# First pass of a graph kernel on Trainium2: ScalarE's norm of the older group ahead of the newer group's root, VectorE's statistics ahead of the scores

## The chip, the cores and the metric

The kernel runs on one core of one Trainium2 chip. Its engines are TensorE (PE), VectorE (DVE), ScalarE (ACT), GpSimd (POOL) and SyncE (SP); each takes its own instructions strictly in their order, and they meet only at semaphores. ACT, POOL and SP also issue DMA transfers. The metric is the device time of one execution in microseconds (us); the time before is the median of three runs.

## The reference, cut to what matters

```python
# x: (50000, 256) f32, 12500 edges (src, dst), dst sorted
h = einsum(x, W); a_src = sum(h * att_src); a_dst = sum(h * att_dst)
e = leaky_relu(a_src[src] + a_dst[dst])            # per edge and head
alpha = softmax of e over the edges with the same dst
gat = relu(segment_sum(h[src] * alpha, dst) + bias)
x1 = layernorm(x + gat)                            # all 50000 rows
for l in range(3):                                 # edges only: 12500
    e = relu((x1[dst] - x1[src]) @ theta.T + x1[src] @ phi.T)
    agg = segment_max(e, src); x1' = relu(batchnorm(agg))
out = layernorm(x1 + x1')
```

Most of the 50000 rows have no edge that ends in them. For these gat is relu(bias), and x1 is layernorm(x + relu(bias)). The first pass computes that for all rows; rows with edges are overwritten later.

## The kernel before

The rows of x are worked in 40 groups, numbered 0 to 39: 39 of 1280 rows (a tile of 128 partitions x 10 rows x 256 features, 1280 KB) and one of 80 rows. The edges are worked in 25 tiles of 512 (`NS` = 25). The part of the program that the change touches runs from about 108 to 404 us, and interleaves the two.

Edge tile t: POOL gathers its dst and src rows with 8 indirect DMAs (L835, function `gat_pool`) into one of two buffers; PE transposes them (L850, `turn`), ACT copies the four banks to SBUF (L879, `gat_keep`), PE multiplies them to the scores (L862, logits) and to h (L868), DVE copies the scores out of PSUM (L895, `gat_score`), SP stores them (L903), and ACT copies h (L888, `gat_keep_h`). PE runs `turn(t+1)` and then the products of tile t; the products of tile t wait for the score copy of tile t - 1, since both use bank 4. POOL may fill a buffer for tile t when tile t - 2 has been transposed (and its dst rows stored by SP).

Row group g: `pre_stats` on DVE waits for the group's load, adds the bias (L778, 128x2560), takes ten bn_stats (L781) and ten bn_aggr (L787). `pre_std` on ACT takes the root (L795). `pre_finish` on DVE makes the inverse root with a Newton step and the shift (L804 to L812). `pre_turnover` on ACT norms the ten rows (`pre_norm`, L820), issues the store (L713) and then the load (L699) of a later group into the ring. Groups 4 to 11 lie in the big buffer and were loaded at the start. All others pass a ring of four buffers: from group 12 on, the turnover of group g issues the load of group g + 3, so the load of group g + 1 goes out behind the norm of group g - 2. The load waits for the store of group g - 1, the ring buffer's last user; the issuing engine, ACT, does that wait.

The order is written out by hand. Step t of the loop pairs edge tile t with group 4 + t: group 28 goes with tile 24, the last. On ACT a step s holds `gat_keep(s)`, `gat_keep_h(s-1)`, `pre_std(4+s-1)` and `pre_turnover(4+s-2)`, so the root of a group stands ahead of the norm of the group before it. On DVE a step t holds `gat_score(t)`, `pre_finish(4+t-1)` and `pre_stats(4+t)`:

```python
            for t in range(NS):
                gat_score(dve, t)
                if t:
                    pre_finish(dve, PRE_SORT + t - 1)
                pre_stats(dve, PRE_SORT + t)
```

After the last tile the scores go to DRAM and back (L903, L935), and DVE runs the softmax over all edges (from L964 on), with groups 29 to 33 put between its pieces, then groups 34 to 39; after that comes the message stage, in which POOL scatters the finished rows (L1123). These parts follow the loop in the same order on every engine.

Of the kernel before, what the change touches and what calls it, by code (L numbers as in the profile page):

```python
# [21 lines left out]
NS = -(-E // SUP)  # L22
# [29 lines left out]
PRE_SORT = 4  # L52
# [7 lines left out]
def gnn(nc, x, src, dst, w, att_src, att_dst, bias, theta_t, phi_t, gammas, betas, out):  # L60
    ctx = ExitStack()
    with ctx:
# [272 lines left out]
        def in_big(g):  # L335

            return PRE_SORT <= g < PRE_SORT + PRE_BIG

        def ring_use(g):

            return g if g < PRE_SORT else g - PRE_BIG
# [7 lines left out]
        def pre_rows(g):  # L349
            if in_big(g):  # L350
                lo = NS * 2 * SUP - (PRE_SORT + PRE_BIG - g) * PR * D
                return big[:, lo:lo + PR * D].rearrange("p (r f) -> p r f", r=PR)
            return pre[:, ring_use(g) % PRE_RING, :, :]

        def loaded(e, g):
            if in_big(g):
                e.wait_ge(s_big_x[(g - PRE_SORT) * 2 // PRE_BIG], 16)
            else:
                e.wait_ge(s_pre_x[ring_use(g) % PRE_RING], 16 * (ring_use(g) // PRE_RING + 1))
# [7 lines left out]
        def node_rows(g):  # L367

            if g == PG:
                return slice(PG * P * PR, N), PTAIL, 1  # L370
            return slice(g * P * PR, (g + 1) * P * PR), P, PR
# [321 lines left out]
        def pre_load(a, use):  # L693
            g = group_at(use)
            rows, p, r = node_rows(g)
            b, u = use % PRE_RING, use // PRE_RING
            if u:
                a.wait_ge(s_pre_stored[b], 16 * u)
            a.dma_start(pre[0:p, b, 0:r, :], x[rows, :].rearrange("(p r) f -> p r f", r=r)).then_inc(s_pre_x[b], 16)  # L699
# [9 lines left out]
        def pre_store(a, g):  # L709
            rows, p, r = node_rows(g)  # L710
            stored = s_big_stored[g - PRE_SORT] if in_big(g) else s_pre_stored[ring_use(g) % PRE_RING]
            a.wait_ge(s_pre_normed, g + 1)
            a.dma_start(x1_dram[rows, :].rearrange("(p r) f -> p r f", r=r), pre_rows(g)[0:p, 0:r, :]).then_inc(stored, 16)  # L713
# [48 lines left out]
        def newtons(g):  # L762

            return 5 * g if g <= PRE_SORT else 5 * PRE_SORT + 4 * (g - PRE_SORT)
# [8 lines left out]
        def pre_stats(v, g):  # L773
            rows, p, r = node_rows(g)
            e, c = g % 2, g - PRE_SORT
            y = pre_rows(g)[0:p, 0:r, :]
            loaded(v, g)
            v.tensor_tensor(y, y, rbias_ps[0:p, :].unsqueeze(1).to_broadcast([p, r, D]), ALU.add).then_inc(s_pre_sum, 1)  # L778
            v.wait_ge(s_pre_sum, c + 1)
            for n in range(r):  # L780
                m = v.bn_stats(stat[0:p, e, n, :], y[:, n, :])  # L781
            m.then_inc(s_pre_stat, 1)
            v.wait_ge(s_pre_stat, c + 1)
            if g > 1:
                v.wait_ge(s_pre_std, g - 1)
            for n in range(r):
                m = v.bn_aggr(mv[0:p, e, n, :], stat[0:p, e, n, :])  # L787
            m.then_inc(s_pre_mv, 1)

        def pre_std(a, g):  # L790
            rows, p, r = node_rows(g)
            e = g % 2
            a.wait_ge(s_pre_mv, g - PRE_SORT + 1)
            a.wait_ge(s_pre_newton, newtons(g - 1))
            a.activation(std[0:p, e, 0:r], mv[0:p, e, 0:r, 1], ACT.Sqrt, bias=eps_b[0:p, :]).then_inc(s_pre_std, 1)  # L795
# [18 lines left out]
        def pre_norm(a, g):  # L814
            rows, p, r = node_rows(g)
            b = g % PRE_RING
            a.wait_ge(s_pre_shift, 2 * g + 2)
            for n in range(r):
                o = pre_rows(g)[0:p, n, :]
                m = a.activation(o, o, ACT.Identity, scale=inv[0:p, b, n:n + 1], bias=shift[0:p, b, n:n + 1])  # L820
            m.then_inc(s_pre_normed, 1)
# [50 lines left out]
        def gat_keep(a, t):  # L872
            par = t % 2
            if t > 1:
                a.wait_ge(s_logits, t - 1)
                a.wait_ge(s_h_done, 2 * (t - 1))
            for n in range(4):
                a.wait_ge(s_row_turned, 4 * t + n + 1)
                a.activation(turned[:, par, 1 - n // 2, n % 2, :], bank[n], ACT.Copy).then_inc(s_row_kept, 1)  # L879
# [10 lines left out]
        def gat_score(v, t):  # L890
            par = t % 2
            v.wait_ge(s_logits, t + 1)
            if t > 1:
                v.wait_ge(s_score_stored[par], 16 * (t // 2))
            v.tensor_copy(score[:, par, :], bank[4][0:H, :]).then_inc(s_score, 1)  # L895
# [637 lines left out]
        @block.sync  # L1533
        def _(sp):
            setup_sync(sp)
            big_load_sync(sp)
            lists_sync(sp)
            soft_masks_sync(sp)
            for s in range(NS + 1):
                if s < NS:  # L1540
                    xd_store(sp, s)
                if 1 <= s <= NS:
                    score_store(sp, s - 1)
            soft_in_sync(sp)
            alpha_sync(sp)
            theta_sync(sp)
            in_steps([(0, lambda t: msg_load(sp, t))], NS)
            for l in range(L):
                conv_sync(sp, l)
            final_sync(sp)  # L1550
            dense_sync(sp)
# [12 lines left out]
        @block.scalar  # L1564
        def _(act):
            act.wait_ge(s_ids, 32)
            for use in range(PRE_SORT):
                pre_load(act, use)
            act.wait_ge(s_const, CONST)

            def pre_turnover(g):
                pre_norm(act, g)
                pre_store(act, g)
                if not in_big(g) and ring_use(g) and ring_use(g) - 1 + PRE_RING < RING_USES:
                    pre_load(act, ring_use(g) - 1 + PRE_RING)
            rows_sum_act(act, 0)
            rows_square_act(act, 0)
            for g in range(1, PRE_SORT):
                rows_sum_act(act, g)
                pre_turnover(g - 1)  # L1580
                rows_square_act(act, g)
            pre_turnover(PRE_SORT - 1)
            act.wait_ge(s_params, PARAMS)
            for s in range(NS + 2):
                if s < NS:
                    gat_keep(act, s)
                if 1 <= s <= NS:
                    gat_keep_h(act, s - 1)
                    pre_std(act, PRE_SORT + s - 1)
                if 2 <= s:  # L1590
                    pre_turnover(PRE_SORT + s - 2)
            for g in range(EARLY, PG + 1):
                if g == EARLY + 2:
                    soft_exp_act(act)
                pre_std(act, g)
                pre_turnover(g)
            msg_act(act)
            for l in range(L):
                conv_act(act, l)
                norm_act(act, l)  # L1600
            final_act(act)
            dense_act(act)

        @block.vector
        def _(dve):
            keys_dve(dve)
            row_bias_dve(dve)
            sort_dve(dve)
            lists_dve(dve)
            rows_finish(dve, PRE_SORT - 1)  # L1610
            rbias_dve(dve)
            weights_dve(dve)
            first_dve(dve)
            for t in range(NS):
                gat_score(dve, t)
                if t:
                    pre_finish(dve, PRE_SORT + t - 1)
                pre_stats(dve, PRE_SORT + t)
            g = EARLY
            soft_flags_dve(dve)  # L1620
            soft_rows_dve(dve)

            def one_group():
                nonlocal g
                pre_finish(dve, g - 1)
                pre_stats(dve, g)
                g += 1
            soft_max_1(dve)
            one_group()
            soft_max_2(dve)  # L1630
            one_group()
            soft_max_3(dve)
            one_group()
            soft_sum_1(dve)
            one_group()
            soft_sum_2(dve)
            one_group()
            soft_sum_3(dve)
            while g <= PG:
                one_group()  # L1640
            pre_finish(dve, PG)
            theta_dve(dve)
            msg_dve(dve)
            for l in range(L):
                conv_dve(dve, l)
                norm_dve(dve, l)
            last_state_dve(dve)
            final_dve(dve)
            dense_dve(dve)
# [46 lines left out]
```

## Time and profile before

| | us |
|---|---|
| median of 3 runs | 1903.24 |
| lowest, highest | 1900.97, 1904.25 |
| profiled execution, its own time | 1906.59 |
| its span (first to last instruction) | 1904.4 |
| VectorE busy | 1296.8 (68%) |
| TensorE busy | 1146.7 (60%) |
| GpSimd busy | 999.6 (52%) |
| ScalarE busy | 946.1 (50%) |

The profiled execution took 1906.59 us, 3.35 us over the median of the runs; its span is 2.2 us shorter than its own time. No engine is busy all through, since the stages have different limits, so the busy shares of the whole span say little about one stage. The stage of the change is some 300 us of the 1904. To read it one needs the waits inside it and the chain of work that ended last, which starts from the last instruction and goes back from each to what released it. A start time in such a row is in us from the start of the span.

### The profile page before, as it was taken

The numbers are of one execution on the slowest core, as the hardware profiler recorded it, in microseconds if no ns is written. First come the engines' busy times: TensorE is split into PE (matmuls) and PEld (weight loads), VectorE is DVE, ScalarE is ACT, GpSimd is POOL, SyncE is SP. The second block draws the span as 40 slices with busy tenths as digits, with TensorE's granted clock in tenths as the row PEclk, the third lists the DMA queues.
The fourth block names the chain that finished last, engine by engine and source line by source line (L and its number), as shares of the span: only waits on it lengthen the run. The fifth ranks groups of instructions, "written<-read, shape, count | busy, mean of one in ns | idle before, by whom it ended". The sixth has DMA issues, their size and how long they took to land.

```text
span 1904.4 us, 16962 instructions
## 1 busy us (share of the span) xinstructions
PE 1146.7 (60%) x3863; PEld 586.0 (31%) x3863; DVE 1296.8 (68%) x3084; ACT 946.1 (50%) x2450; POOL 999.6 (52%) x1032
## 2 busy tenths in 40 slices
PE   0159888840047772799998598997999893000000
PEld 0023333310023331455554344553444451000000
DVE  8837867689879994245554345554666687778887
ACT  4726777765432222244443355563555454555664
POOL 1067766677637777777772773424544067730000
PEclk9999999975555555799999799998999897555555
DMA  9367899977844542588885377756766278999997
GB/s 358 126 194 244 290 359 361 349 244 248 276 140 147 161 162 94 170 258 263 260 260 165 88 155 173 189 159 133 145 141 134 87 237 306 374 357 351 347 346 306
DMA packets 177391, 436.12 MB, mean 229 GB/s; under 512 B 28804, under 2 KB 108810, under 8 KB 157324
## 3 DMA queue, kind: packets, MB, share of 16 engines
q1 hardware_dynamic: 109020, 229.52, 35.4%
q0 software_dynamic: 44800, 100.49, 21.0%
q10 hardware_dynamic: 23472, 105.03, 15.2%
q8 instruction: 32, 0.52, 0.1%
q14 instruction: 67, 0.55, 0.1%
HBM read 257.16 MB, written 182.32 MB: 231 GB/s over the span
## 4 chain that ended last, share of the span: by engine, by line
PE 35%; DVE 21%; DMA 17%; POOL 11%; issue 8%; ACT 6%; SPq 1%; ACTq 0%; POOLq 0%; DVEq 0%
DMA arena<-x 12%; PE ps L1245 12%; PE ps L1258 12%; POOL x L1123 4%; PE ps L1235 4%; DVE arena L1508 3%; POOL slot L678 3%; DVE arena L1491 3%; ACT arena L820 3%; DVE stat L781 3%; PE ps L1422 2%; POOL arena L1198 2%; DVE arena L778 2%; PE ps L1274 2%; POOL arena L1216 1%
## 5 line engine op out<-in xcount | busy, mean ns | idle before, releaser
L1330 DVE TENSOR_TENSOR_SCAN arena<-arena,ps 128x512 f32<-128x512 f32 x150 | 190.7, 1276 | 273.5 <-PE ps L1245 242.0
L1216 POOL DMA_INDIRECT arena<-agg,slot x200 | 188.9, 945 | 205.7 <-PE ps L1235 109.8
L835 POOL DMA_INDIRECT arena<-x,idx x200 | 189.7, 948 | 172.2 <-DVE idx L601 91.0
L1258 PE MATMUL ps<-arena 128*128 128x512 f32 x600 | 273.8, 600 | 8.9 <-ACT arena L1300 8.9
L1245 PE MATMUL ps<-arena 128*128 128x512 f32 x600 | 276.0, 603 | 5.0 <-DVE arena L1330 5.0
L1522 ACT ACTIVATE arena<-arena 128x256 f32<-128x256 f32 x391 | 156.5, 401 | 141.4 <-DVE arena L1491 141.4
L1198 POOL DMA_INDIRECT arena<-x,idx x200 | 189.1, 946 | 62.0 <-issue 59.1
L820 ACT ACTIVATE arena<-arena,shift,inv 128x256 f32<-128x256 f32 (+1 forms) x311 | 156.1, 587 | 51.6 <-DVE shift L812 34.8
L1334 DVE TENSOR_TENSOR ps<-arena,ps 128x512 f32<-128x512 f32 x150 | 103.9, 695 | 104.8 <-PE ps L1258 104.8
L1087 PE MATMUL ps<-arena,head_of 8*128 8x512 f32 x100 | 93.7, 1088 | 124.6 <-DVE arena L1042 88.0
L1459 POOL DMA_INDIRECT x<-big,idx x100 | 121.1, 1211 | 87.6 <-DVE big L1449 55.1
L1235 PE MATMUL ps<-ident,arena 128*128 128x128 f32 x800 | 112.1, 286 | 88.1 <-DMA arena<-x,idx 45.1
L1258 PEld LDWEIGHTS ps<-arena 128*128 128x128 f32 x600 | 115.3, 193 | 154.4 <-issue 145.0
L1300 ACT ACTIVATE arena<-big,bn_shift,bn_scale 128x512 f32<-128x512 f32 x100 | 76.0, 807 | 164.4 <-PE ps L1258 154.4
L1491 DVE TENSOR_TENSOR arena<-arena 128x2560 f32<-128x2560 f32 (+1 forms) x40 | 110.6, 2764 | 56.3 <-DMA arena<-x 56.2
L1245 PEld LDWEIGHTS ps<-arena 128*128 128x128 f32 x600 | 111.1, 195 | 116.8 <-issue 116.6
L1293 ACT ACTIVATE arena<-ps 128x512 f32<-128x512 f32 x100 | 54.7, 595 | 169.0 <-PE ps L1235 169.0
L678 POOL DMA_INDIRECT slot<-slot_of,idx x100 | 97.9, 979 | 70.8 <-issue 63.2
L1235 PEld LDWEIGHTS ps<-ident,arena 128*128 128x128 f32 x800 | 95.1, 147 | 110.9 <-issue 56.9
L1123 POOL DMA_INDIRECT x<-big,idx x100 | 99.7, 997 | 55.0 <-issue 30.7
L685 POOL DMA_INDIRECT slot_of<-slot_of_pos,idx x100 | 105.9, 1059 | 30.5 <-issue 30.5
L1508 DVE TENSOR_SCALAR arena<-arena,inv 128x256 f32<-128x256 f32 x391 | 110.7, 359 | 1.4
(211 smaller groups left out, 2190.5 us busy)
## 6 DMA issues: line engine op xcount, KB each, us to landing
arena<-x SPq DMA_DIRECT2D x39, 1280.0 KB, 7.9
out<-arena SPq DMA_DIRECT2D x39, 1280.0 KB, 5.4
arena<-x ACTq DMA_DIRECT2D x31, 1280.0 KB, 10.5
x<-arena ACTq DMA_DIRECT2D x31, 1280.0 KB, 6.4
agg<-arena SPq DMA_DIRECT2D x50, 512.0 KB, 4.2
arena<-not_same SPq DMA_DIRECT2D x75, 256.0 KB, 4.9
arena<-last_of SPq DMA_DIRECT2D x75, 256.0 KB, 6.1
x_dst<-arena SPq DMA_DIRECT2D x25, 512.0 KB, 3.8
```

The lines of the kernel that those rows point to most:

```text
L820: m = a.activation(o, o, ACT.Identity, scale=inv[0:p, b, n:n + 1], bias=shift[0:p, b, n:n + 1])
L835: pl.indirect_dma_start(rows_in[:, par, a, g, :], None, x[:, :], bass.IndirectOffsetOnAxis(ap=idx[:, k, t * G + g:t * G + g + 1], axis=0)) ...
L1123: pl.indirect_dma_start(x1_dram[:, :], bass.IndirectOffsetOnAxis(ap=idx[:, D_END, t * G + g:t * G + g + 1], axis=0), x1_big[:, t, g, :], N ...
L1198: pl.indirect_dma_start(conv_in[:, b, a, g, :], None, x1_dram[:, :], bass.IndirectOffsetOnAxis(ap=idx[:, k, t * G + g:t * G + g + 1], axis ...
L1216: pl.indirect_dma_start(conv_in[:, b, 1, g, :], None, agg_dram[l - 1][:, :], bass.IndirectOffsetOnAxis(ap=slot[:, t * G + g:t * G + g + 1] ...
L1235: m = pe.transpose(turn_bank[j][:, g * P:(g + 1) * P], conv_in[:, b, a, g, j * P:(j + 1) * P], ident[:, :])
L1245: m = pe.matmul(far_bank[j], thp[:, l, 0, k, j * P:(j + 1) * P], far_t[:, par, k, :], start=(k == 0), stop=(k == 1))
L1258: m = pe.matmul(near_bank[j], thp[:, l, 1, k, j * P:(j + 1) * P], near_t[:, par, k, :], start=(k == 0), stop=(k == 1))
L1330: v.tensor_tensor_scan(runmax[:, par, j, :], mask[:, tl % 2, :], far_bank[j], initial, ALU.add, ALU.max).then_inc(s_conv_scan, 1)
L1491: v.tensor_tensor(y, y, c_rows[0:p, :].unsqueeze(1).to_broadcast([p, r, D]), ALU.add).then_inc(s_dense_y, 1)
L1508: m = v.tensor_scalar(o, o, inv[0:p, g % 2, n:n + 1], None, ALU.mult)
L1522: m = a.activation(unused[0:p, n, :], y_tile[0:p, b, n, :], ACT.Square, scale=1.0 / ROOT, accum_out=msq[0:p, b, n:n + 1])
```

## The change

On ACT the turnover of the older group (norm, store issue, load issue) now stands ahead of the root of the newer one in each of the steps 2 to 25. On DVE the statistics of group 4 + t now stand ahead of the score copy of tile t and of the Newton step of group 4 + t - 1. No instruction is added or removed, PE, POOL and SP keep their order, and the waits on semaphores keep their values.

```diff
                     gat_keep_h(act, s - 1)
-                    pre_std(act, PRE_SORT + s - 1)
                 if 2 <= s:
                     pre_turnover(PRE_SORT + s - 2)
+                if 1 <= s <= NS:
+                    pre_std(act, PRE_SORT + s - 1)
...
             for t in range(NS):
+                pre_stats(dve, PRE_SORT + t)
                 gat_score(dve, t)
                 if t:
                     pre_finish(dve, PRE_SORT + t - 1)
-                pre_stats(dve, PRE_SORT + t)
```

VectorE at the start of the loop, the piece of the difference: L895 copies a tile's scores, L778 to L787 are a group's statistics, L804 to L812 its Newton step.

```order
 L671 TENSOR_SCALAR tiles_needed<-tiles_f 1x40
-L895 COPY score<-ps 8x512
 L778 TENSOR_TENSOR big<-big,ps 128x2560
 L781 BN_STATS stat<-big 128x6 x10
 L787 BN_AGGR mv<-stat 128x2 x10
 L895 COPY score<-ps 8x512
-L804 RECIPROCAL ps<-std 128x10
-L806 SCALAR_TENSOR_TENSOR step<-mv,ps 128x10
-L807 SCALAR_TENSOR_TENSOR ps<-mv,ps 128x10
-L809 SCALAR_TENSOR_TENSOR step<-step,ps 128x10
-L811 SCALAR_TENSOR_TENSOR inv<-step,ps 128x10
-L812 SCALAR_TENSOR_TENSOR shift<-step,ps 128x10
```

The first group's statistics need no score any more, and from there on each score copy and Newton step has one group's statistics more ahead of it than before.

VectorE at the end of the loop, where the last score copy (tile 24) and the masks of the softmax (L911, L912) stand:

```order
 L781 BN_STATS stat<-arena 128x6 x10
 L787 BN_AGGR mv<-stat 128x2 x10
+L895 COPY score<-ps 8x512
+L804 RECIPROCAL ps<-std 128x10
+L806 SCALAR_TENSOR_TENSOR step<-mv,ps 128x10
+L807 SCALAR_TENSOR_TENSOR ps<-mv,ps 128x10
+L809 SCALAR_TENSOR_TENSOR step<-step,ps 128x10
+L811 SCALAR_TENSOR_TENSOR inv<-step,ps 128x10
+L812 SCALAR_TENSOR_TENSOR shift<-step,ps 128x10
 L911 TENSOR_SCALAR arena<-arena 128x800
```

The L787 here is that of group 28: the last score copy now comes behind the statistics of group 28, where before it came ahead of them.

## Rows read from the trace of the kernel before

**Rows 1.** Stretches: us, PE, PEld, DVE, ACT, POOL busy, clock, DMA share, GB/s

```profile
130.00:240.00 110.00, 98.69 (x331) 41.31 (x329) 85.56 (x282) 76.49 (x154) 83.19 (x89) 0.97 0.75 253
240.00:400.00 160.00, 130.92 (x422) 55.32 (x422) 113.40 (x385) 116.20 (x236) 110.20 (x116) 0.93 0.96 346
```

**Rows 2.** Chain that ended last, 187 to 208 us: start, duration, engine and line

```profile
187.13 0.21 DVE ps L804
...
188.00 2.74 DVE big L778
...
201.41 2.04 PE ps L850 x16
...
207.02 0.04 DVE score L895
...
207.63 0.21 DVE ps L804
```

**Rows 3.** POOL in order of time: start, duration, in brackets the idle time before

```profile
125.92 0.94 POOL L835 DMA_INDIRECT arena<-x,idx  x1 [6.35 <-DMA x_dst<-arena]
...
269.05 0.94 POOL L835 DMA_INDIRECT arena<-x,idx  x1 [3.45 <-PE ps L850]
```

**Rows 4.** Chain that ended last, 298 to 324 us

```profile
298.65 11.64 DMA arena<-x
...
310.32 2.83 DVE arena L778
...
317.38 0.30 ACT std L795
317.68 4.92 ACT arena L820 x10
...
323.00 9.57 DMA arena<-x
```

**Rows 5.** ACT in order of time: issues of the loads of groups 16, 18, 26, 28

```profile
250.86 0.88 ACTq L699 DMA_DIRECT2D arena<-x  x1
...
275.69 0.46 ACTq L699 DMA_DIRECT2D arena<-x  x1
...
368.56 0.45 ACTq L699 DMA_DIRECT2D arena<-x  x1
...
393.55 0.58 ACTq L699 DMA_DIRECT2D arena<-x  x1
```

**Rows 6.** Time to landing of a group's load (L699)

```profile
DMA to landing us min/median/max: 8.1/10.4/16.0
```

**Rows 7.** Time to landing of a gather (L835)

```profile
DMA to landing us min/median/max: 2.7/4.6/9.8
```

**Rows 8.** DVE in order of time: score copies of tiles 10 and 24, statistics of 26 and 28

```profile
236.43 0.68 DVE L895 COPY score<-ps 8x512 f32<-8x512 f32 x1 [0.49 <-PE ps L862]
...
380.88 2.82 DVE L778 TENSOR_TENSOR arena<-arena,ps 128x2560 f32<-128x2560 f32 x1 [2.31 <-DMA arena<-x]
...
402.55 0.68 DVE L895 COPY score<-ps 8x512 f32<-8x512 f32 x1 [4.88 <-PE ps L862]
...
403.95 2.81 DVE L778 TENSOR_TENSOR arena<-arena,ps 128x2560 f32<-128x2560 f32 x1
```

**Rows 9.** PE in order of time: products to h of tile 10

```profile
236.33 3.70 PE L868 MATMUL ps<-arena,w_sb 128*128 128x512 f32 x8
```

**Rows 10.** ACT in order of time: the two copies of h

```profile
244.10 1.29 ACT L888 ACTIVATE big<-ps,bias_t 128x512 f32<-128x512 f32 x2
```

**Rows 11.** Chain that ended last, 400 to 418 us

```profile
403.26 7.53 DMA scores<-score
...
410.80 5.19 DMA arena<-scores
```

**Rows 12.** Waits from 240 to 400 us: total us, times, longest us

```profile
DVE arena L778 <- DMA arena<-x: 21.6, 13, 3.2
```

**Rows 13.** POOL in order of time: first scatter of the message stage

```profile
564.88 1.02 POOL L1123 DMA_INDIRECT x<-big,idx  x1 [24.37 <-ACT big L1114]
```

## Prediction

> **What bounds the kernel now.** First the busy time by stretches, for where the loop's limits lie. From 130 to 240 us the DMA engines are busy for 0.75 of the time and no engine is full; from 240 to 400 us their share is 0.96 at 346 GB/s [rows 1]. So there are two halves, and each needs its own chain. Then the chain that ended last, in each half.
>
> In the first half (edge tiles 0 to 10, groups 4 to 14) the chain comes back to the same place, a Newton step, after 207.63 - 187.13 = 20.50 us, which is two steps of the loop: Newton step, statistics of the next group, its root on ACT, the norm of the older group behind that root, the copies of a tile on ACT, transposes and scores on PE, the score copy, Newton step; four of its stations and its two ends are shown [rows 2]. 10.25 us a step. Beside it POOL issues 112 gathers (tiles 2 to 15) from 125.92 to 265.60 without a gap longer than its own, 9.98 us for the 8 of a tile [rows 3]. POOL is thus the floor, 0.27 us a step below the chain.
>
> In the second half the chain runs through the ring: load of a group, its statistics, its root, the norm of the older group behind it, the issue of the next load but one [rows 4]. From the load of group 16 at 250.86 to that of group 28 at 393.55 it goes round six times, 23.78 us each [rows 5]. From the start of the statistics at 310.32 to the next issue at 323.00 are 12.68 us [rows 4], so the loads take 23.78 - 12.68 = 11.10 us in the mean. VectorE waits 21.6 us for loads there [rows 12], and from 265.60 on POOL waits for PE [rows 3]: GpSimd is no floor here.
>
> Behind the loop nothing gives a shift back. The softmax starts when the scores are back from DRAM, VectorE is in one row of work from there to the message stage, and POOL's first scatter comes after 24.37 us of idling for a normed tile [rows 13]. What the last score copy gains or loses, the end gains or loses.
>
> **The change part by part.** ACT's half of the edit takes the root off the norm's way: the norm of group g - 1 no longer stands behind the statistics of group g on ACT. But the norm also waits for its own Newton step, and VectorE's half puts that step behind the statistics of group g and the score copy. So the norm of g - 1 still comes after the statistics of g, by another path.
>
> *First half.* That path does no harm here, because groups 4 to 14 are loaded in time, and VectorE's step is short: statistics 317.38 - 310.32 = 7.06 [rows 4], score copy 207.63 - 207.02 = 0.61, Newton step 188.00 - 187.13 = 0.87 [rows 2], 8.54 us in sum, against POOL's 9.98. The 20.50 us chain is gone, since statistics no longer wait for a score. What is late next is POOL. Tile 11's last gather is issued at 125.92 + 10 x 9.98 - 0.3 = 225.4 and lands at the earliest 2.7 us later [rows 3, 7], 228.1; the last transposes (about a quarter of 2.04) and the scores of tile 10, 207.02 - 201.41 - 2.04 = 3.57, put its score copy at about 232.2 [rows 2], where it was at 236.43 [rows 8]. Its h products end 3.70 us after the scores, 235.9 [rows 9], the two copies on ACT take 1.29 [rows 10], and then the norm of group 13 and the store's issue (323.00 - 317.68 = 5.32 [rows 4]) put the load of group 16 at 242.5 instead of 250.86. It lands 11.1 later, at 253.6; statistics, score copy and Newton step (8.54), norm and issue (5.32) give the load of group 18 at 267.5 instead of 275.69 [rows 5]. **Term 1: -8.2 us.** Its ends are 0, if POOL's gathers land late enough to eat the lead (a gather's median is 4.6, its slowest 9.8 [rows 7]), and about -10.
>
> *Second half.* The loop from a load to the next but one is now: load, statistics 7.06, score copy 0.61, Newton step 0.87, norm and issue 323.00 - 317.68 = 5.32 [rows 2, 4]: 13.86 us beside the load, where 12.68 stood. The root, 0.30 us, left the loop; the score copy and the Newton step came in: +1.18 us each time round. The load's own time is open. The loads now come in pairs about 10 us apart, as POOL's pace left them, with a longer gap behind, where they were about 11.8 apart; each brings a store and a load of 1280 KB onto engines that are 0.96 busy [rows 1]. Ends: no change, 11.1, or the 12.32 that a load took in this stretch, issued at 368.56 and waited for until 380.88 [rows 5, 8]. I take 0.7 us more, near the 11.64 of the load in rows 4. From group 18 to group 28 it goes round five times: 5 x (1.18 + 0.7) = **Term 2: +9.4 us** (5.9 to 12.0).
>
> *The end of the loop.* Before, the last score copy started 402.55 - 393.55 = 9.00 us after the issue of group 28's load, ahead of that group's statistics, which began without waiting 1.4 us later [rows 5, 8]. Now it stands behind them. The load had landed by 10.4 us after its issue, the median is 10.4 too and the fastest 8.1 [rows 6]; with 7.0 us of statistics the copy starts 17.4 us after the issue (15.1 to 19.3). **Term 3: +8.4 us** (6.1 to 10.3). VectorE gets no time back for statistics done early: before, it did them and the masks inside the 410.80 + 5.19 - 403.26 = 12.7 us that the scores spent going to DRAM and back [rows 11], and now it idles there.
>
> *The scores' way.* Those 7.53 us for 16 KB fell just behind a store and a load issued on ACT at the same time. Now the copy need not meet them. Between 0 and -4 us; I take **Term 4: -1.0 us**.
>
> The score copy also frees bank 4. Behind it on PE queue the products of the next tile and its h. They take 3.57 + 3.70 [rows 2, 9] and are wanted only a step of about 12 us later, so I cost it at nothing; without that cover it would be a few tenths a step. SP's store of the dst rows stands behind the score's store, and is wanted two tiles later: nothing. ACT's store and load issues move ahead of the root with the norm, together 6 us each step; the root is wanted by VectorE only behind 7 us of statistics: nothing.
>
> The Trainium skill's page "DMA: Bandwidth & Descriptors", section "Issuing engines are not separate DMA queues", says that transfers of all issuing engines run on the same 16 DMA engines and interleave. It speaks against reading the earlier loads as free; the DMA share of 0.96 [rows 1] agrees with it. By it alone term 2 would lie at its upper end, and the time at 1914.
>
> Sum: -8.2 + 9.4 + 8.4 - 1.0 = +8.6 us, so 1906.6 + 8.6 = 1915.2 for an execution like the profiled one. That one took 3.35 us more than the median of the runs, and I take that as its own; against the median 1903.2 + 8.6 gives **1911.8**.
>
> **The rivals.** *A: the pace is the transfers'.* If the loads' time is mostly queueing for DMA engines that are full, a longer loop just finds shorter queues, and the pace of 23.6 us for two groups stays. For it: 0.96 busy [rows 1]. Against: VectorE's start after each landing sets the next issue, and 13 waits of 1.7 us in the mean show that each load is waited for by itself [rows 12]. Then term 2 is 0 and the sum is -0.8: 1902. The same page states, in its section "Specifications", an HBM limit of about 358 GB/s for a core; the 346 GB/s of rows 1 lie close under it and agree with it. My chance for A rests on the share and the waits of rows 1 and 12 alone.
>
> *B, the other side: the early lead stays.* The loads spread, each takes the fastest time seen, 8.1 us [rows 6], and the loop is 21.96 us: term 2 is 5 x (21.96 - 23.57) = -8.0, term 3 is 6.1, the scores save 2: -8.2 - 8.0 + 6.1 - 2 = -12.1, 1891. It decides from a load time below about 9.4 us. Against: a store and a load are 2.6 MB, and 2.6 MB at 346 GB/s is already 7.6 us without any gather.
>
> *C: the pairs collide.* Loads in pairs take 12.3 us and more, and the norm also waits on ACT for the copies of h now that it stands just behind them, up to 1.3 us each time round: term 2 is 5 x (1.18 + 1.2 + 1.3) = +18.4, term 3 +10.3, term 4 zero: +20.5, 1924; half of it gives 1917.
>
> *D: the first half does not speed up.* POOL's floor or the first tiles' late start keep the loads where they are; term 1 is -3 instead of -8.2: 1917.
>
> **How the numbers follow.** The forecast with its own spread, 1907 to 1916, has 0.45. C and D together 0.25 (1916 to 1924). A has 0.20 (1899.5 to 1907). B has 0.10, spread from 1891 to 1899. The range that leaves out half of B and the top of C is 1899 to 1921. This kernel's measurements can tell about 0.2%, 3.8 us, from no change: faster by more 0.10, within 0.20, slower 0.70. Most likely time 1912.
>
> **What would show it.** In the changed kernel's profile: the first statistics (L778) start near 108 us and not at 131; no wait of the root (L795) for statistics up to 240 us; the load of group 16 near 243 us and VectorE's waits for loads (L778) far more than 21.6 us in all; from there about 25.5 us from a load's issue to the next but one; the last score copy near 411 us, behind group 28's statistics, and VectorE idle for some 5 us before the softmax's first instruction (L964). Term 1 is wrong if group 16's load comes at 248 or later, term 2 if two groups take under 24.3 or over 26.5 us, term 3 if the last score copy starts less than 15 us after the issue of group 28's load. Were the first part wrong as well, and the loads of both halves early, the kernel would be faster than before.

## The result and the profile after

| | before | after |
|---|---|---|
| median | 1907.35 us (21 runs) | 1915.76 us (21 runs) |
| lowest to highest | 1900.97 to 1912.23 us | 1904.51 to 1923.74 us |
| profiled execution: time, span | 1906.59, 1904.4 us | 1915.88, 1913.7 us |

The ratio after/before is 1.0042, 95% interval 1.0027 to 1.0058: slower, by 8.4 us between the medians. The forecast was +8.6 us. The sum came true; the terms did not all do so, and most of what follows is on that. The medians are over all executions; an execution over 1.5% above its kernel's fastest, like one of 2837.82 us of ACT's half below, is left out of the ratios.

The 21 executions of the changed kernel spread over 19 us, and six of them took 1904.51 to 1908.11 us, as little as the kernel before. The profile is of one at 1915.88 us, near the median. What follows on the single terms holds for that execution; how the six fast ones avoid the loss no trace shows.

The stretches first, columns as in [rows 1]:

```profile
130.00:240.00 110.00, 99.39 (x339) 41.53 (x337) 83.86 (x281) 82.12 (x165) 83.17 (x89) 0.97 0.77 261
240.00:400.00 160.00, 131.25 (x407) 52.74 (x408) 107.36 (x364) 108.17 (x218) 102.29 (x108) 0.87 0.95 343
```

ACT gets a little further up to 240 us (165 instructions for 154), and the engines do less from there to 400 (VectorE 364 instructions for 385, GpSimd 108 for 116, ACT 218 for 236).

ACT in order of time, the issues of the loads of groups 16, 18, 20, 26 and 28, against [rows 5]:

```profile
244.21 0.45 ACTq L699 DMA_DIRECT2D arena<-x  x1
...
269.26 0.48 ACTq L699 DMA_DIRECT2D arena<-x  x1
...
293.74 0.44 ACTq L699 DMA_DIRECT2D arena<-x  x1
...
364.26 0.45 ACTq L699 DMA_DIRECT2D arena<-x  x1
...
388.61 0.46 ACTq L699 DMA_DIRECT2D arena<-x  x1
```

Group 18's load is 6.4 us earlier than before (269.26 for 275.69), group 28's 4.9 us (388.61 for 393.55). Up to there the changed kernel is ahead; what it loses, it loses in the 40 us behind group 28's load.

DVE in order of time, the score copy of tile 10, the statistics of groups 18, 26 and 28, and the last score copy, against [rows 8]:

```profile
234.59 0.68 DVE L895 COPY score<-ps 8x512 f32<-8x512 f32 x1 [1.49 <-PE ps L862]
...
279.88 2.82 DVE L778 TENSOR_TENSOR arena<-arena,ps 128x2560 f32<-128x2560 f32 x1 [1.69 <-DMA arena<-x]
...
374.48 2.82 DVE L778 TENSOR_TENSOR arena<-arena,ps 128x2560 f32<-128x2560 f32 x1 [0.76 <-DMA arena<-x]
...
402.10 2.82 DVE L778 TENSOR_TENSOR arena<-arena,ps 128x2560 f32<-128x2560 f32 x1 [2.28 <-DMA arena<-x]
...
409.04 0.65 DVE L895 COPY score<-ps 8x512 f32<-8x512 f32 x1
```

PE's products of tile 24 to its scores:

```profile
400.62 3.60 PE L862 MATMUL ps<-arena,v_att 128*8 128x512 f32 x8
```

Then the chain that ended last, from the score copy of tile 21 by the load of group 28 to the softmax, against [rows 11]:

```profile
372.35 0.57 DVE score L895
...
373.06 5.90 PE ps L862 x8
...
382.62 0.69 ACT big L888
383.31 4.91 ACT arena L820 x10
...
388.61 13.46 DMA arena<-x
...
402.10 2.83 DVE arena L778
...
409.13 0.57 DVE score L895
...
409.71 7.77 DMA scores<-score
...
417.50 10.43 DMA arena<-scores
...
428.03 1.00 DVE arena L964
```

The softmax's first instruction (L964) starts at 428.03 where it started at 416.08: 11.95 us late. It has two predecessors: the scores back from DRAM, and VectorE's own row (statistics of group 28, masks). Before, VectorE waited 0.24 us for the scores, so its row was ready at 415.84; now it waits 12.39 us and was ready at 428.03 - 12.39 = 415.64. So the whole delay at L964 is that of the scores. GpSimd's first scatter of the message stage, against [rows 13], is 11.2 us late:

```profile
576.09 1.02 POOL L1123 DMA_INDIRECT x<-big,idx  x1 [26.24 <-ACT big L1114]
```

The span is 9.3 us longer. So 2.7 us of the 11.95 came back behind L964; single executions of one kernel differ by more, and I can't say whether the order had a part in it.

Waits from 240 to 430 us (total us, times, longest us); before, L778 waited 21.6 us there, L835 for x_dst 0.6 us, and L862 for the score copy was not in the list:

```profile
DVE arena L778 <- DMA arena<-x: 56.8, 14, 8.6
...
POOL arena L835 <- DMA x_dst<-arena: 19.5, 7, 7.4
...
PE ps L862 <- DVE score L895: 12.3, 4, 3.4
```

### The profile page after: what moved, and what is told of

Read it like the earlier page. It is cut to its first block, busy times and chain, and to the rows that moved or that the text cites. A ratio compares the mean times of both kernels' runs of the same rounds, so it can differ in the third digit from the quotient of the medians.

```text
span 1913.7 us, 16962 instructions
## 1 busy us (share of the span) xinstructions
PE 1151.7 (60%) x3863; PEld 584.8 (31%) x3863; DVE 1295.9 (68%) x3084; ACT 947.0 (49%) x2450; POOL 1002.8 (52%) x1032
## 4 chain that ended last, share of the span: by engine, by line
PE 31%; DMA 19%; DVE 19%; POOL 16%; issue 10%; ACT 4%; SPq 1%; ACTq 0%; POOLq 0%; DVEq 0%
DMA arena<-x 12%; PE ps L1245 11%; PE ps L1258 11%; POOL x L1123 4%; POOL arena L1198 3%; PE ps L1235 3%; POOL slot L678 3%; DVE arena L1508 3%; DVE arena L1491 3%; POOL arena L835 3%; ACT arena L820 2%; DVE stat L781 2%; POOL arena L1216 2%; DMA arena<-x,idx 2%; DVE arena L778 2%
## 5 line engine op out<-in xcount | busy, mean ns | idle before, releaser
L835 POOL DMA_INDIRECT arena<-x,idx x200 | 190.3, 951 | 182.6 <-DVE idx L601 90.9
L685 POOL DMA_INDIRECT slot_of<-slot_of_pos,idx x100 | 106.4, 1064 | 30.5 <-issue 30.5
L778 DVE TENSOR_TENSOR arena<-arena,ps 128x2560 f32<-128x2560 f32 (+1 forms) x28 | 76.5, 2732 | 60.2 <-DMA arena<-x 60.2
```

The source lines that it names most:

```text
L835: pl.indirect_dma_start(rows_in[:, par, a, g, :], None, x[:, :], bass.IndirectOffsetOnAxis(ap=idx[:, k, t * G + g:t * G + g + 1], axis=0)) ...
```

## The experiments

All ratios are to the kernel before on the same chip, with 95% intervals. The kernel before took 1906.9 us (25 runs) beside the first four. Start times are from the one profiled execution of each.

**Each half alone.** The change has two halves: on ACT `pre_turnover` ahead of `pre_std`, on VectorE `pre_stats` ahead of `gat_score`. First ACT's half:

```diff
                 if 1 <= s <= NS:
                     gat_keep_h(act, s - 1)
-                    pre_std(act, PRE_SORT + s - 1)
                 if 2 <= s:
                     pre_turnover(PRE_SORT + s - 2)
+                if 1 <= s <= NS:
+                    pre_std(act, PRE_SORT + s - 1)
```

> ScalarE's half of the edit alone: the norm of the older group ahead of the newer one's root; VectorE keeps its order (score copy, Newton step, statistics). Theory 1, it is VectorE's order that costs: the norm of group g - 1 now waits for nothing behind the statistics of group g, a round of the ring spans three groups (11.1 load + 7.06 + 0.3 + 0.87 + 5.32 = 24.7 us, 8.2 us a group), so POOL's 9.98 us or the transfers set the pace, the last score copy comes 10 to 20 us earlier than before's 402.6, and the kernel is 10 to 20 us faster than before. Theory 2, the transfers set the pace of the second half whatever the order: the loads' time grows instead, the pace stays near 11.8 us a group, and the kernel gains only the first half's lead, 6 to 8 us.

Measured: 1912.83 us, 1.0035 [1.0016, 1.0055]. My theory of the moment, a gain of 10 us and more, fell. ACT's issues of its loads (L699) show what happened:

```profile
329.92 0.44 ACTq L699 DMA_DIRECT2D arena<-x  x1
...
339.14 0.69 ACTq L699 DMA_DIRECT2D arena<-x  x1
...
359.19 0.45 ACTq L699 DMA_DIRECT2D arena<-x  x1
...
368.42 0.45 ACTq L699 DMA_DIRECT2D arena<-x  x1
...
386.49 0.44 ACTq L699 DMA_DIRECT2D arena<-x  x1
```

The loads run 9.2 us apart in bursts, and then there is none for 18 to 20 us. Its waits from 240 to 430 us, and GpSimd in one of the stops:

```profile
DVE score L895 <- PE ps L862: 42.5, 9, 10.3
...
PE ps L850 <- DMA arena<-x,idx: 29.8, 9, 7.0
...
POOL arena L835 <- DMA x_dst<-arena: 21.6, 5, 9.8
...
DVE arena L778 <- DMA arena<-x: 1.7, 2, 1.2
```

```profile
353.03 0.95 POOL L835 DMA_INDIRECT arena<-x,idx  x1 [8.26 <-DMA x_dst<-arena]
```

Hardly any wait for loads is left. Instead PE waits for gathers and GpSimd for x_dst, and through them VectorE for the scores. The GpSimd row is from the stop between 339 and 359 us; a store of x_dst lands after 4.6 us in the median and 11.6 at most here, after 3.8 and 8.6 before.

The loss has two parts of like size. Group 28's statistics start at 408.18 instead of 403.95, since its load goes out and lands later, and the last score copy at 404.71, 2.2 us late. Then the load of the scores takes 11.1 us for 5.2, and VectorE waits 4.05 us for it: L964 starts at 424.36, 8.3 us late. The medians differ by 5.9.

VectorE's half:

```diff
             for t in range(NS):
+                pre_stats(dve, PRE_SORT + t)
                 gat_score(dve, t)
                 if t:
                     pre_finish(dve, PRE_SORT + t - 1)
-                pre_stats(dve, PRE_SORT + t)
```

> VectorE's half alone: statistics ahead of score copy and Newton step; ScalarE keeps root before norm. Theory 1: the norm's wait is the Newton step behind the statistics, whichever of the two stands first on ScalarE, so this takes the time of the whole change within 2 us: 7 to 11 us slower than before. Theory 2 (the halves add up, ScalarE's half gives a gain of its own in the whole change): slower than the whole change by 5 us or more.

Measured: 1918.63 us, 1.0052 [1.0031, 1.0073]: as slow as the whole change or a little slower (the two intervals overlap). VectorE's waits for loads are 60.1 us from 240 to 400 us, against 54.6 in the whole change. With statistics ahead of score and Newton step it matters little what ACT does with the root.

**VectorE's order with ACT's new one.** `gat_score` put back ahead of `pre_stats`, with `pre_finish` last:

```diff
             for t in range(NS):
-                pre_stats(dve, PRE_SORT + t)
                 gat_score(dve, t)
+                pre_stats(dve, PRE_SORT + t)
                 if t:
                     pre_finish(dve, PRE_SORT + t - 1)
```

> The whole change, but on VectorE the score copy stands ahead of the statistics again, the Newton step stays behind them. Theory 1 (the last score copy's place costs the most): the ring's round stays as in the changed kernel (about 23.9 us for two groups), the last score copy comes some 9 us after the issue of group 28's load instead of 20.4, and the kernel is within 4 us of before, 8 to 14 us faster than the change. Theory 2 (the Newton step's place costs): still over 5 us slower than before.

Measured: 1906.24 us, 0.9997 [0.9980, 1.0014]. One line's place takes away the whole loss, as theory 1 has it. Its last score copy starts at 402.77 (before 402.55, after 409.04) and L964 at 416.88 (before 416.08, after 428.03). So the loss comes from the score copy behind the statistics, in the loop or at its end or both.

More than the last copy has moved back, though. The load of group 18 goes out at 275.27 (before 275.69, after 269.26), and five rounds from there to group 28's, at 392.96, take 23.54 us each, not the 23.9 that I expected to stay: the whole loop is back at the times of before. The scores are back at 411.0, and L964 does not wait for them; it comes at the end of VectorE's own row. And GpSimd waits 25.3 us for stores of x_dst here, more than the 19.5 in the whole change, with no loss in time: such waits alone are no sign of one.

The Newton step first and the score copy last:

```diff
             for t in range(NS):
-                pre_stats(dve, PRE_SORT + t)
-                gat_score(dve, t)
                 if t:
                     pre_finish(dve, PRE_SORT + t - 1)
+                pre_stats(dve, PRE_SORT + t)
+                gat_score(dve, t)
```

> The whole change, but on VectorE the Newton step stands ahead of the statistics, the score copy stays behind them. Theory 1: the ring's rounds get shorter, but each score copy waits for a load and 7 us of statistics; the last one still starts 15 us or more after the issue of group 28's load, so most of the gain of the first half is spent: within 5 us of before. Theory 2 (the Newton step's place is what costs): as fast as ScalarE's half alone.

Measured: 1946.01 us, 1.0222 [1.0200, 1.0244]. I had it within 5 us of before; a miss by 34 us. The chain that ended last shows why, here from 293 to 340 us:

```profile
293.17 6.17 DMA arena<-x,idx
...
299.38 1.09 PE ps L850 x8
300.47 3.53 PE ps L862 x8
304.00 3.65 PE ps L868 x8
...
308.36 4.92 ACT arena L820 x10
...
314.66 0.31 ACT std L795
...
315.90 2.74 DVE arena L778
...
322.84 0.57 DVE score L895
...
323.75 5.39 DMA x_dst<-arena
...
329.21 8.55 DMA arena<-x,idx
...
337.80 1.97 PE ps L850 x8
```

This is one ring through everything: gathers, transposes, h products, norm, root, Newton step, statistics, score copy, then on SP the store of x_dst, which stands behind the score's store, then the next gathers. VectorE waits 53.7 us for the root from 240 to 400 us, and 3.7 us for loads in all. With the Newton step at the head of VectorE's row the score copy waits for ACT's root as well as for the statistics, and ACT's root waits, by way of the copies of h and the norm, for the scores' tile.

**Is the second half paced by the transfers?** The kernel before, and ACT's half alone, each with a fifth of the bytes of the loads of groups 16 to 28:

```diff
+            w = 2 if 16 <= g <= 28 else r
-            a.dma_start(pre[0:p, b, 0:r, :], x[rows, :].rearrange("(p r) f -> p r f", r=r)).then_inc(s_pre_x[b], 16)
+            a.dma_start(pre[0:p, b, 0:w, :], x[rows, :].rearrange("(p r) f -> p r f", r=r)[:, 0:w, :]).then_inc(s_pre_x[b], 16)
```

> The kernel before, with one edit: the loads that ScalarE issues for groups 16 to 28 carry 2 of the 10 rows of each partition, so the tiles built from these groups hold old rows in the rest (the output is then not that of the reference). Asked: whether the second half of the first pass (240 to 400 us) is paced by the transfers. In the kernel before their share is 0.96 there, the loads are issued every 11.8 us in the mean, and GpSimd waits 7.3 us in all for stores of x_dst. Theory 1 (the transfers set the pace): with a fifth of the bytes of these loads the pace falls to the 9.98 us a tile of GpSimd or little above, the last score copy comes near 380 instead of 402.6, and the span falls by 15 to 22 us. Theory 2 (the chain of engines sets it, the transfers only fill): the pace stays above 11.3 us a tile and the last score copy comes after 395.

> The ScalarE half of the change alone, with the same edit of the loads of groups 16 to 28 (2 of 10 rows of a partition; the output is then not that of the reference). The ScalarE half alone took 5.9 us more than the kernel before, with its loads in pairs 9.2 us apart and then a gap of 15 to 20 us, and with GpSimd waiting 21.6 us for stores of x_dst. Theory 1 (the loads in pairs hold up the gathers and the x_dst stores behind them): with a fifth of the bytes there is nothing to hold up, the wait of GpSimd for stores of x_dst in 240 to 400 us is under 6 us, and the kernel is within 2 us of the kernel before with the same edit, or faster. Theory 2 (the order of ScalarE itself makes the loop longer, whatever the transfers): it stays 5 us or more above that kernel, with the pairs and gaps as they were.

| | median, us | ratio to before | last score copy | L964 |
|---|---|---|---|---|
| before, small loads | 1894.05 | 0.9925 [0.9898, 0.9952] | 386.50 | 399.99 |
| ACT's half, small loads | 1891.52 | 0.9914 [0.9883, 0.9945] | 380.95 | 397.55 |

(The kernel before took 1908.41 us on this chip.) In the first, the waits from 240 to 430 us are these (lines 1 higher than before):

```profile
DVE score L896 <- PE ps L863: 32.2, 12, 5.8
...
POOL arena L836 <- DMA x_dst<-arena: 8.9, 5, 3.7
...
DVE arena L779 <- DMA arena<-x: 1.7, 1, 1.7
```

In the second:

```profile
DVE score L896 <- PE ps L863: 20.7, 9, 7.6
...
PE ps L851 <- DMA arena<-x,idx: 13.2, 6, 4.1
...
POOL arena L836 <- DMA x_dst<-arena: 3.4, 4, 1.9
```

The transfers do pace the second half in good part: with a fifth of the bytes of these loads the kernel before is 14.4 us faster, just under the 15 to 22 us of theory 1. But the chain of engines lies close below. From tile 10's score copy at 234.77 to tile 24's at 386.50 it is 10.84 us a tile, between the 11.87 of before and the 9.98 of GpSimd; my 380 was too early. In ACT's half the waits for x_dst went from 21.6 to 3.4 us, and the kernel that was 0.35% above before is now 2.5 us below before with the same loads, a difference that the two intervals can't tell from none. Its loss is gone with the bytes, as theory 1 has it: the norm's earlier place does not cost by itself, but through the transfers. Which of the transfers carries the loss is less plain than I wrote in the expectation. About half of it at L964 was the scores' load, which lands after 6.3 us here for 11.1 with full loads. For the half in the loop, a store of x_dst took 7.4 us in the median with the small loads and 4.6 with the full ones, and was yet waited for less; the gathers, with PE's wait of 13.2 us for 29.8, fit better.

**Six runs that could not answer.** On two other chips the kernel before itself took 2290.36 us (31 runs) and 2284.74 us (23 runs). The last tiles of the first pass are then held up by something that no order of mine touches. Here is the stretch from 400 to 600 us in the second run of the kernel with the last score copy moved (columns as in [rows 1]), and its last two score copies and L964 on DVE:

```profile
400.00:600.00 200.00, 44.43 (x94) 15.09 (x92) 51.57 (x157) 43.90 (x88) 125.09 (x128) 0.60 0.29 88
```

```profile
523.99 0.68 DVE L895 COPY score<-ps 8x512 f32<-8x512 f32 x1 [69.85 <-issue]
568.08 0.68 DVE L895 COPY score<-ps 8x512 f32<-8x512 f32 x1 [42.60 <-remote]
585.40 0.99 DVE L964 SCALAR_TENSOR_TENSOR arena<-arena 128x800 f32<-128x800 f32 x1
```

In the six profiles L964 comes at 576.6 to 599.0 us, whatever stood behind what before it. The edits, all on the changed kernel: for the last tile alone, score copy and Newton step ahead of statistics, as in `if t == NS - 1: gat_score; pre_finish; pre_stats` (run twice);

> The whole change, but in the last step of the loop (tile 24, group 28) VectorE keeps the old order: score copy, Newton step, statistics. Theory 1 (the last score copy behind group 28's statistics costs 8 to 11 us, its place in the other 24 steps little): the last score copy at about 400 us instead of 409, the scores back in SBUF near 414, and the kernel 8 to 14 us faster than the whole change, that is 0 to 5 us faster than before. Theory 2 (score copies behind loads delay the tiles all along): the gain on the whole change is under 4 us.

> The whole change, but in the last step of the loop VectorE keeps the old order: score copy of tile 24, Newton step, statistics of group 28. On a chip where the kernel before takes about 1907 us. Theory 1 (the last score copy's place behind group 28's statistics is what the change pays, 8 to 11 us): last score copy within 12 us of the issue of group 28's load instead of 20.4, the kernel 5 to 12 us faster than the whole change, that is within 4 us of before. Theory 2 (score copies behind loads delay the tiles all along): under 4 us faster than the change.

VectorE's order Newton step, score copy, statistics in every step;

> ScalarE's half of the edit, and on VectorE Newton step, score copy, statistics. Theory 1 (transfers set the pace; norms that come earlier issue loads in clusters, and the edge tiles' gathers and stores of dst rows are what then lands late): the same picture as with ScalarE's half alone, loads 9.2 us apart in clusters with gaps of 15 us and more, POOL waiting for stores of dst rows; 2 to 8 us slower than before. Theory 2 (the score copy ahead of the Newton step is what holds the ring up there): 8 us or more faster than before.

on SP, the score's store one step later, behind the store of x_dst (`if 2 <= s <= NS: score_store(sp, s - 2)`, the last one after the loop);

> The whole change, and SyncE stores the scores of a tile one step later, so that the store of the dst rows of tile s + 1 no longer stands behind the score copy of tile s - 1, which VectorE's new order makes late. Theory 1 (SyncE's queue is the way by which late score copies hold up POOL): POOL's waits for stores of dst rows, 26.3 us in the changed kernel, fall under 10, and the kernel is 3 to 8 us faster than the change. Theory 2 (these stores are late because the DMA engines are full): the waits stay over 15 us and the time within 3 us of the change.

and at s == NS the pair of store and load held back by `act.wait_ge(s_scores_in, 16)` until the scores are back (run twice).

> The whole change, and ScalarE holds the store of group 27 and the load of group 30, which it issued at 415.6 and 415.9 us, until the scores are back in SBUF. Theory 1 (the scores' way took 18.2 us after the last score copy's issue instead of 12.7 because their 400 KB load met that pair): the load lands within 6 us of its issue instead of 10.4, the softmax starts 13 to 15 us after the last score copy instead of 19, and the kernel is 3 to 5 us faster than the change. Theory 2 (it was POOL's scatter of slots, or chance): no change.

> The whole change, and ScalarE holds the store of group 27 and the load of group 30 until the scores are back in SBUF. On a chip where the kernel before takes about 1907 us. Theory 1 (the scores' load of 400 KB took 10.4 us because it met that pair): it lands within 6 us of its issue, the softmax starts 13 to 15 us after the last score copy instead of 19, and the kernel is 3 to 5 us faster than the change. Theory 2 (the scatters of slots or chance made it late): no change.

The ratios to the kernel before on those chips: last copy moved, 1.0010 [0.9963, 1.0057] and 0.9985 [0.9944, 1.0025]; Newton step, score copy, statistics, 1.0001 [0.9954, 1.0047]; score's store one step later, 0.9970 [0.9929, 1.0011]; pair held back, 0.9996 [0.9956, 1.0037] and 1.0050 [1.0020, 1.0079]. The changed kernel was not run there, and nothing follows from any of them for the other chips.

How much of the loss is the last copy's place alone, and what a held pair would give back, stay untested. For the first the trace of the changed kernel gives a bound. PE had the scores of tile 24 at 400.62 + 3.60 = 404.2, 1.7 us later than before (402.5), and the copy started at 409.04: group 28's statistics held it up by at most 4.8 us. So of the 11.95 us at L964 up to 4.8 are the last copy's place as such, 1.7 the tile's own lateness, and 5.5 the way by DRAM. Whether a copy at 404.2 would have spared those 5.5 too no run shows.

## Why the prediction came out, step by step

| L964 against before | predicted, us | measured, us |
|---|---|---|
| term 1, load of group 18 | -8.2 | -6.4 |
| term 2, five rounds of the ring | +9.4 | +1.5 |
| term 3, load 28's issue to last score copy | +8.4 | +11.4 |
| term 4, scores to DRAM and back | -1.0 | +5.5 |
| sum | +8.6 | +12.0 |

**What bounds the kernel** was right in its outline, with two exceptions. "What the last score copy gains or loses, the end gains or loses" holds for losses alone: VectorE's own row was ready 0.24 us before the scores, so a gain of the copy by itself would have stopped there. And the 346 GB/s of [rows 1] are a mean and no ceiling: slices of 4 us in that stretch reach 419 GB/s, in the changed kernel 431. The first L778 starts at 107.61, and from 130 to 240 us the root no longer waits for statistics; its waits are short ones for ACT itself, 4.9 us in all.

**Term 1** had the mechanism and 1.8 us too much: tile 10's copy came at 234.59 for 232.2, mostly since I gave the last gather its fastest landing, 2.7 us (PE went on with it at 229.93, not 228.1). Rival D is out.

**Term 2 is the step that failed.** Its first part was right: from the statistics of group 18 at 279.88 to the issue at 293.74 are 13.86 us, the sum that the prediction made; over the five rounds it is 13.91 in the mean for 12.67 before, +6.2 us. The second part had the wrong sign. I gave each load 0.7 us more. A load waited for took 9.96 us in the mean (first 279.88 - 269.26 = 10.62) for 10.90 of the same five groups before: 5 x -0.94 = -4.7 us. A round is 119.35 / 5 = 23.87 us, below the 24.3 that I had named as the bound of the term. That is rival A's mechanism, most but not all of it, and the experiment with small loads supports its premise: the transfers held the pace up by 1.9 us in two steps. (Loads issued from 270.75 for group 18 to 379.25 for group 28 there: 21.70 us a round for 23.57.) I had set against A that each load is waited for by itself. That is no argument: a wait for one transfer says nothing on how much of its time is queueing. Why the loads got shorter in this order no run separates. The Trainium skill's page "DMA: Bandwidth & Descriptors", section "Issuing engines are not separate DMA queues", has all issuers' transfers run on the same 16 DMA engines and interleave. The run of the kernel before with small loads agrees: only ACT's loads were cut, and GpSimd's gathers from 240 to 400 us landed after 4.6 us in the median for 8.0. By it I had put term 2 at its upper end, and the sharing worked the other way.

**Term 3** had the order right and the load too short. The copy starts 20.43 us after load 28's issue: statistics 409.04 - 402.10 = 6.94, as predicted, behind a load of 13.49 instead of 10.4. Of the +11.4 us some 3.1 are the load's. Of the step itself the traces show that the copy was held: PE had the scores at 404.2, 4.8 us ahead of it. The kernel with the score copy put back supports it too, but moves the copy in every tile.

**Term 4** had the wrong sign. I looked at one pair of store and load, the one that the store of the scores met before. In the changed kernel that store met a pair again (7.77 for 7.53 us), and the load of the scores met another one, issued 1.6 us ahead of it: 10.43 for 5.19 us. VectorE idles for it:

```profile
428.03 0.99 DVE L964 SCALAR_TENSOR_TENSOR arena<-arena 128x800 f32<-128x800 f32 x1 [12.39 <-DMA arena<-scores]
```

I had said 5 us.

**What I costed at nothing.** PE does wait for bank 4 (12.3 us), and GpSimd for x_dst's stores (19.5), whose median landing went from 3.8 to 8.4 us. Each was said to have cover. The chain that ended last, shown with the result, does go by bank 4 in the last round: score copy of tile 21, products of tile 22, copies of its h, norm, load of group 28. But the ring was nearly as late there: group 26's statistics at 374.48 and 13.86 us give 388.34 for that load, and it went out at 388.61, so the way by bank 4 costs 0.27 us over the ring. Further back, in rows not shown, the chain goes by the gathers of tile 12 (8.86 us to landing) and the copies of h into the load of group 17, issued at 260.03 where the ring's sum gives 243.84 + 13.86 = 257.70. None of GpSimd's waits for x_dst behind 240 us lies on it. So "nothing" was off by tenths in this execution, since the other groups' half of the ring was only 0.27 us ahead; in the kernel with the Newton step first SP's store of x_dst stands on the path beyond doubt. A cover of a few us should have been worked out, not assumed.

**The total.** Term 2 was 7.9 us too high; terms 1, 3 and 4 were 1.8, 3.0 and 6.5 too low, 11.3 together. At L964 the sum was 3.4 us short, and the end gave back 2.7. That the medians differ by 8.4 for 8.6 forecast is luck: the direction, the lead of the first half and the late last copy were foreseen, but errors of 1.8 to 7.9 us in the four terms cancelled for the most part, and the 2.7 us behind L964 took off most of the rest. Between 1912 and the measured 1915.76 stands mostly the base: I started from 1903.24, the median of three runs, where 21 give 1907.35. The profiled execution, forecast at 1915.2, took 1915.88.

## What to carry to other kernels

When work is moved ahead of a short copy whose result others wait for, price three places: the loop, the loop's last round, where nothing hides the copy's delay, and the way of its result through DRAM, where it can meet transfers that it did not meet before. Where two paths join (here the scores and VectorE's own row, 0.24 us apart), read both: the later one alone sets the time, so a delay on it costs in full and a lead soon gains nothing. A load's time in a stretch where the DMA engines are 0.96 busy isn't a constant to multiply: here a longer loop was largely paid for by shorter loads, and loads in bursts by later gathers and a later load of the scores. A root or norm taken off an engine's queue gains nothing where the same result waits for the same data by way of another engine.

## What the runs showed that I had not expected

A small transfer took longer here when large ones had been issued just ahead of it. Over eight executions: the time from the start of the last score copy to the issue of the scores' load on SP (a store of 16 KB in between), and the time to landing of that load (400 KB); beside them how long ahead ACT had issued its last load, of 1280 KB but for the mark, which has a store of 1280 KB just ahead of it. A minus sign means that it came behind:

| kernel | copy to load's issue, us | ACT's load, ahead of copy | load's landing, us | ACT's load, ahead of it |
|---|---|---|---|---|
| before | 8.25 | -0.8 | 5.2 | 7.5 |
| after | 8.46 | 2.3 | 10.4 | 1.6 |
| ACT's half | 8.41 | -0.5 | 11.1 | -0.2 |
| VectorE's half | 9.48 | 1.6 | 10.4 | 2.3 |
| Newton step first, score last | 8.23 | 1.3 | 4.7 | 9.6 |
| score first | 3.62 | 9.8 | 4.6 | 13.4 |
| before, small loads | 3.42 | 7.3 (256 KB) | 4.3 | 10.7 (256 KB) |
| ACT's half, small loads | 8.54 | -0.6 | 6.3 | 7.9 |

Some 3.5 us for the store without a pair within 7 us ahead and 8.2 to 9.5 with one; 4.3 to 6.3 us for the load without, 10.4 to 11.1 with. The split has no exception in these eight, but it is read off, not made: the runs that were to move the pair fell on the other chips, and gathers and other transfers differ between the rows too.

And the same program took 20% longer on two other chips: 2290 us for 1907, some 170 us of it between 400 and 600 us, while GpSimd's small scatters (L685) run and the DMA engines do little (a share of 0.14 and 41 GB/s from 440 to 570 us in the profile above). What holds the engines there the profile calls only "issue" or "remote". It is open.
